# Prologue of an attention and FFN kernel: order of the bias loads, eps and mean on VectorE, and identity transposes in the first microseconds

## The reference

```python
x = x + _layernorm(attn(_layernorm(x), w_qkv, b_qkv, w_o, b_o))
x = x + _layernorm(ffn(_layernorm(x), W, b, A, B, gate_w, gate_b))

def _layernorm(x, eps=1e-05):
    return (x - mean(x)) / sqrt(var(x) + eps)

# attn: 8 heads of 64
qkv = x @ w_qkv.T + b_qkv
scores = einsum('bhfc,bhtc->bhft', k, q)           # causal, masked with -10000
vals = einsum('bhft,bhfc->bhtc', softmax(scores, axis=-2), v)
out = vals @ w_o.T + b_o
# ffn: x @ W.T + b, plus a low-rank product whose rank (8, 16, 32, 64) a gate picks for each row
```

## Time and profile before

| | us |
|---|---|
| median of 3 runs | 1416.98 |
| lowest, highest run | 1416.22, 1417.29 |
| the profiled execution | 1418.16 |
| its span, first to last instruction | 1416.3 |
| TensorE busy in the span | 1397.8 (99%) |
| VectorE, ScalarE, GpSimd busy | 1039.4, 693.1, 704.2 |

### The profile page before, as it was taken

The page is one execution under the profiler, slowest core; times in us unless marked ns, Lnnn a source line. Parts: engine busy times, 40 slices in busy tenths (PEclk is TensorE's granted clock), DMA queues, the critical chain, the costliest instruction groups (busy, mean ns, idle before and its releaser), DMA issues.

```text
span 1416.3 us, 24933 instructions
## 1 busy us (share of the span) xinstructions
PE 1397.8 (99%) x7796; PEld 1249.5 (88%) x7796; DVE 1039.4 (73%) x2204; ACT 693.1 (49%) x1498; POOL 704.2 (50%) x1268
## 2 busy tenths in 40 slices
PE   7999999999999999999999999999999999999998
PEld 6888888888888888888888889999999999999998
DVE  7676675775775776766756788888887787787774
ACT  6365465564564664644655763333333333333332
POOL 3363562562562553635624684555555555555542
PEclk9999999999999999999999999999999999999999
DMA  7334234234233342342232743222223222222321
GB/s 252 127 97 128 108 97 142 89 102 139 93 111 107 109 133 103 96 141 100 93 97 93 213 142 112 95 101 104 98 95 104 104 96 90 93 91 104 116 77 60
DMA packets 68774, 157.54 MB, mean 111 GB/s; under 512 B 7425, under 2 KB 31233, under 8 KB 68737
## 3 DMA queue, kind: packets, MB, share of 16 engines
q1 hardware_dynamic: 68736, 157.08, 33.3%
HBM read 62.15 MB, written 25.69 MB: 62 GB/s over the span
## 4 chain that ended last, share of the span: by engine, by line
PE 89%; POOL 4%; issue 3%; POOLq 2%; ACT 1%; DVE 0%; DMA 0%; DVEq 0%; SPq 0%; ACTq 0%
PE ps_f L2409 23%; PE ps_o L1483 21%; PE ps_o L1514 12%; PE ps_o L2331 6%; PE ps_s L1534 6%; PE ps_v L1358 5%; PE ps_t L1396 3%; PE ps_o L1477 3%; PE ps_z L2331 2%; PE ps_f L2389 2%; PE ps_o L1437 2%; PE ps_x L2379 1%; PE ps_v L1366 1%; POOL wagl L609 1%; PE ps_o L1495 1%
## 5 line engine op out<-in xcount | busy, mean ns | idle before, releaser
L2409 PE MATMUL ps_f<-wagh,x2Th 128*128 128x364 f32 x768 | 254.7, 332 | 0.6 <-DVE x2Tl L846 0.6
L2409 PE MATMUL ps_f<-wagh,x2Tl 128*128 128x364 f32 x768 | 252.5, 329 | 0.0
L2409 PE MATMUL ps_f<-wagl,x2Th 128*128 128x364 f32 x768 | 252.1, 328 | 0.0
L1483 PE MATMUL ps_o<-xTh,wh 128*128 128x512 f32 x424 | 172.2, 406 | 0.0
L1483 PE MATMUL ps_o<-xTh,wl 128*128 128x512 f32 x424 | 166.1, 392 | 0.0
L1483 PE MATMUL ps_o<-xTl,wh 128*128 128x512 f32 x424 | 165.3, 390 | 0.0
L572 POOL TENSOR_SCALAR pr<-pr,nwm,rden 128x512 f32<-128x512 f32 (+3 forms) x256 | 159.1, 636 | 11.3 <-issue 11.3
L548 POOL TENSOR_TENSOR cw<-wm,cnt 128x4 f32<-128x4 f32 x64 | 12.8, 200 | 301.7 <-ACT pr L1122 301.7
L2409 PEld LDWEIGHTS ps_f<-wagh,x2Th 128*128 128x128 f32 x768 | 144.2, 188 | 2.6 <-DVE x2Tl L846 0.8
L2409 PEld LDWEIGHTS ps_f<-wagl,x2Th 128*128 128x128 f32 x768 | 144.5, 188 | 1.6
L2409 PEld LDWEIGHTS ps_f<-wagh,x2Tl 128*128 128x128 f32 x768 | 144.4, 188 | 0.0
(11 more groups left out here) (303 smaller groups left out, 3412.2 us busy)
## 6 DMA issues: line engine op xcount, KB each, us to landing
p_words<-pr SPq DMA_DIRECT2D x56, 448.0 KB, 2.8
kst<-kst SPq DMA_DIRECT2D x64, 256.0 KB, 3.7
x<-in_x SPq DMA_DIRECT2D x31, 512.0 KB, 3.4
x2r<-x2n SPq DMA_DIRECT2D x30, 512.0 KB, 2.9
xs<-in_x SPq DMA_DIRECT2D x24, 512.0 KB, 4.6
out<-x SPq DMA_DIRECT2D x23, 512.0 KB, 2.6
p_words<-pr SPq DMA_DIRECT2D x56, 192.0 KB, 2.3
valsT<-vt SPq DMA_DIRECT2D x64, 128.0 KB, 2.3
```

The costliest lines, as they stand in the source:

```text
L1483: done = pe.matmul(ps[:, :], w[:, k, c:c + P], xT[:, k, :], start=(k == 0 and w is wh and xT is xTh), stop=(k == KD - 1 and w is wl), skip ...
L2409: last = pe.matmul(ps_f[:, g, 0:GW], a[:, k, :], w[:, k, cols], start=(k == 0 and a is xh and w is wagh), stop=False, skip_group_check=True)
```

## The change

Four edits, all in the prologue:

1. SP issues the two bias loads behind five weight chunks, where it did so behind three.
2. VectorE adds eps to the variance (a scalar addition behind a second drain), and for tile 0 negates the mean too; mv_ready now comes from the eps addition. GpSimd begins with the power.
3. GpSimd normalises tiles 1 to 3 by subtracting the mean that the statistics hold, where it added the negated mean. A function normalise_first stands for the first batch, and layernorm remains for the others.
4. TensorE transposes the identity 18 times before the first x tile. Of the eight such transposes behind tile 3 four remain.

```diff
-            for n in range(3):
+            for n in range(RAW):
                 load_w(n)
             sp.dma_start(bqk_s[:, :], bqk).then_inc(bias_landed, 16)
             sp.dma_start(bv_s[:, :], bv).then_inc(bias_landed, 16)
-            for n in range(3, len(W_CHUNKS)):
+            for n in range(RAW, len(W_CHUNKS)):
                 load_w(n)
...
+            def normalise_first(t):
+
+                pool.wait_ge(mv_ready, t + 1)
+                pool.tensor_tensor(rstd[:, t:t + 1], var_eps[:, t:t + 1], mhalf[:, :], ALU.pow)
+                pool.drain()
+                if t == 0:
+                    pool.tensor_tensor(shift0[:, :], nmean[:, t:t + 1], rstd[:, t:t + 1], ALU.mult).then_inc(x0_shift, 1)
+                    return
+                pool.tensor_scalar(x_tile(t, 0), x_tile(t, 0), mv[:, t, 0:1], rstd[:, t:t + 1], ALU.subtract, ALU.mult)\
                     .then_inc(xn_ready, 1)
...
+            def first_stats(t):
+
+                dve.wait_ge(x_landed[t], 16)
+                for i in range(2):
+                    dve.bn_stats(stats[:, t, 6 * i:6 * i + 6], x_half(t, 0, i))
+
+                dve.drain()
+                dve.bn_aggr(mv[:, t, :], stats[:, t, :])
+                dve.drain()
+                if t == 0:
+                    dve.tensor_scalar(nmean[:, 0:1], mv[:, 0, 0:1], -1.0, None, ALU.mult)
+                dve.tensor_scalar(var_eps[:, t:t + 1], mv[:, t, 1:2], EPS, None, ALU.add).then_inc(mv_ready, 1)
...
             pe.wait_ge(ident_turned, 1)
             pe.wait_ge(consts, 15)
+            for _ in range(18):
+                pe.transpose(ps_v[:, 0:P], ident[:, :], ident[:, :])
             for t in range(NT - 1):
                 transpose_x0(t)
...
-            for _ in range(8):
+            for _ in range(4):
                 pe.transpose(ps_v[:, 0:P], ident[:, :], ident[:, :])
```

More of the change, by code:

```diff
@@ L532, in layernorm @@
                 pool.tensor_tensor(nmean[:, q:q + 1], mv[:, q, 0:1], mone[:, :], ALU.mult)
-                pool.wait_ge(ve_done, n + 1)
+                pool.wait_ge(ve_done, n + 1 - NT)
                 pool.tensor_tensor(rstd[:, q:q + 1], var_eps[:, q:q + 1], mhalf[:, :], ALU.pow)
                 pool.drain()
-                if isinstance(b, int) and n == 0:
-                    pool.tensor_tensor(shift0[:, :], nmean[:, q:q + 1], rstd[:, q:q + 1], ALU.mult).then_inc(x0_shift, 1)
-                    return
                 at = x_tile(t, b)
                 pool.tensor_scalar(at, at, nmean[:, q:q + 1], rstd[:, q:q + 1], ALU.add, ALU.mult)\
+                    .then_inc(xn_ready, 1)
+            def normalise_first(t):
[6 more added lines that the diff above has]
+                pool.tensor_scalar(x_tile(t, 0), x_tile(t, 0), mv[:, t, 0:1], rstd[:, t:t + 1], ALU.subtract, ALU.mult)\
                     .then_inc(xn_ready, 1)
@@ L681, in gpsimd @@
             for t in range(NT):
-                layernorm(t, 0)
+                normalise_first(t)
             pool.wait_ge(w_hi, 1)
@@ L1025, in split_w @@
                     .then_inc(w_ready, 1)
-            for t in range(3):
-                layernorm_stats(t, 0)
-            layernorm_stats(3, 0)
+            for t in range(NT):
+                first_stats(t)
             for t in range(NT):
```

## The result

| | before | changed |
|---|---|---|
| median of 6 runs, us | 1416.88 | 1424.6 |
| lowest to highest, us | 1416.22 to 1417.68 | 1423.44 to 1425.4 |
| span of the profiled execution, us | 1416.3 | 1423.6 |

The ratio of the runs is 1.0053, with a 95% interval of 1.0042 to 1.0063. That is 7.7 us, and it lies outside the range of the prediction (1415.6 to 1418.5). The forecast was no difference.

A forecast was written before the change was run, and what follows sets the result against it. TensorE's matmul stream was taken as the bound, movable only at its start. VectorE held by GpSimd gave +0.5 us, identities and biases 0: 1417.5 us on the 1416.98 median, range 1415.6 to 1418.5.

The forecast's parts named there:

- What bounds the kernel: TensorE's unbroken matmul stream from 16.41 us on; the change could only move its start, and that shift reaches every later block.
- the anchor: The stream's last wait, 0.2 us for VectorE's first low half of a weight chunk; its timing follows tile 3's transposes.
- The subtraction in the normalisation: GpSimd's normalisation of x tiles in the prologue: subtract assumed to cost 1.19 us, like the addition.
- anything else: Leftover chance for outcomes outside the held case and rivals A, B and C: 4%.
- GpSimd loses 0.29 us a tile: Dropping eps and negation on GpSimd shortens its period from 2.16 to 1.87 us; 0.4 us to be had at tile 3.
- VectorE becomes the gate of tile 3's transposes: VectorE's added drains and eps delay its low halves of x; unheld, the transposes start at 14.19, 0.14 later.
- Held by GpSimd: VectorE's eps of tile 3 waits out GpSimd's normalisation of tile 2; transposes start at 14.56, +0.5 us; chance 50%.
- rival A: VectorE's single-element eps addition is not held; tile 3's transposes start at 14.19, +0.1 us, 1417.1; chance 25%.
- Identities at no cost and no gain: 18 early identity transposes on TensorE run in idle time, ending at 6.3 us; gain 0.
- Biases at nothing: Bias loads moved later on SP: bounds 0 to -0.36 us on VectorE's start of tile 2, taken as 0.
- D: The DMA dip at 5 to 6 us is unrelated to the biases, so moving them changes nothing; no chance of its own.
- C: Early identities raise TensorE's clock, a thin stretch lets it fall; half speed from 14.05 to 18.1, up to +4 us; 4%.

The follow-up runs named there:

- a_add: The changed kernel with add in place of subtract, VectorE negating every tile's mean: 1417.43 us against 1416.73 for the kernel before, ratio 1.0004.
- h_order: a_add with TensorE's transposes of tile 3 put ahead of the low-half products that wait for VectorE: 1416.79 us against 1416.92 for before, ratio 0.9998.
- q_hold: The kernel before plus ten VectorE additions of 1 to 64 elements beside three GpSimd add/mult operations; one element takes 0.15 us, no kernel time given.
- second trace of before: The kernel before run and traced once more, unchanged, to show the spread between executions: 1416.68 us, one run.

## Why the prediction was wrong, step by step

- **What bounds the kernel, and the way to the anchor: right.** The stream arrives at the last batch with the delay that it had at the start (8.05 us at the anchor; 7.94 or 7.23 at the scores, by the trace of before that it is set against).
- **"The subtraction in the normalisation has the same operands and size as the addition, so 1.19 us as before": this is the step that failed**, and alone decides. It measured 3.79. Three times 2.60 are 7.8 us, of which 7.26 reached the tile, since the rest of GpSimd's chain got shorter. The trace of before had no subtract of this form on GpSimd, and I took the row of another operation for it. No rival had it, so it stood at the 4% for anything else. The one row of a subtraction that I had, in the earlier trace rows, was a warning: that of two tensors of 1024 elements takes 2.39 us, and three normalisations at that price would have been 3.6 us more and outside my range. But it was no bound, since the measured 3.79 lies above it. The price was open, and no row that I had read closed it from above.
- **GpSimd loses 0.29 us a tile: right.** In a_add its period from tile 2 to tile 3 is 12.62 - 10.73 = 1.89 us, where I had 1.87, and in h_order its tile 3 is ready at 13.52.
- **VectorE becomes the gate of tile 3's transposes: right in mechanism**, shown in a_add (0.31 us wait) and by h_order. The eps addition starts 0.28 us behind the start of the aggregate in the changed kernel (11.14 - 10.86), where I had 0.31.
- **Held by GpSimd: wrong.** The eps of tile 3 starts at 11.14, inside GpSimd's normalisation from 8.48 to 12.27, and takes 0.15. It was rival A. The Trainium skill ("SBUF — State Buffer", section "SBUF: two separate sides") has VectorE's two-port mode and GpSimd exclude each other; q_hold agrees with it for 2 and 64 elements (0.70 and 1.03, and 1.07 us), and a single element is outside it (0.15 us). In the Trainium skill the page "VectorE: DVE Perf Modes" (section "Mode 2×_2P — use both read ports for one tensor") asks for an even length, or odd and equal ones, of the outermost dimension that is not one. I took a single element for an odd length; it has no such dimension, so the page did not promise the hold that I gave 50%.
- **Identities at no cost and no gain: right**, though my reading of the pace was too simple: tile 2's transposes are quick without identities in other executions (8 in 1.11 us in the second trace of before).
- **Biases at nothing: right**, and so was D.
- **C, the clock at the lower level: it came, but by another cause.** I put it on the early identities and a thin stretch; it came of TensorE waiting for GpSimd, and cost 0.8 us. The slow pace is there without the identities.

## What to carry to other kernels

An instruction's row prices that operation, not its form: where a change swaps the operation, find a row with the new one on the same engine, or leave the price open in the range: a near row is not an upper bound (here the nearest subtraction took 2.39 us and the new operation 3.79). On GpSimd, write a normalisation as add and mult with a negated mean; here it takes 1.19 us where subtract and mult take 3.79. And where a wait is taken off one engine's path, look which instruction stands ahead of the freed one on the waiting engine: here the products that wait for VectorE, put behind the transposes, gave GpSimd's gain back, some 0.4 us in the trace.

## What the runs showed of the hardware that I had not expected

- GpSimd's tensor and two scalars, 128 x 1024 in float32: 1.19 us for add and mult in either order, 3.79 for each of the four pairs tested with a subtract, 2.84 for a single add and 2.85 for a single subtract.
- VectorE's scalar addition from SBUF to SBUF is held by a busy GpSimd at 2 and at 64 elements a partition (up to 1.03 and 1.07 us), and not at one (0.15 us).
- The granted clock was at 0.50 from 11 to 24 us when TensorE idled 3.1, 2.5 and 1.7 us between groups of transposes, and those of tiles 2 and 3 took 0.25 us each in place of 0.14.
- Two executions of one unchanged kernel differ by 2.8 us from the last batch's scores to the first output product, by 0.8 us on the way there, and by 0.8 us in when VectorE starts on the third x tile (7.91 and 7.13).
